# State-space inputs shifted by one step: from matrix products in the token loop to transfers ahead of it

## The reference, cut to what matters

```python
gamma = lam * dt
beta = (1.0 - lam) * dt * jnp.exp(A_disc)
X = x_heads * gamma[..., None] + jnp.pad(x_heads[:, :-1] * beta[:, 1:, :, None], ((0, 0), (1, 0), (0, 0), (0, 0)))
Y, _ = ssd_chunk(X, A_disc, Bm, Cm)
```

## Time and profile before

| | |
|---|---|
| median of 3 runs | 3973.22 us (3966.16 to 3978.81) |
| the profiled execution | 3973.28 us, its span 3971.5 us |
| PE busy | 3450.7 us, 87% |
| DVE busy | 2610.3 us, 66% |
| ACT busy | 1180.8 us, 30% |
| POOL busy | 503.4 us, 13% |
| mean granted TensorE clock | 0.914 |

### The profile page before, as it was taken

One profiled execution on the slowest core, in us unless ns is written; L12 is line 12 of the kernel. 1 busy time (PEld: TensorE's weight loads), 2 busy tenths in 40 slices (PEclk: granted clock), 3 DMA queues, 4 the chain that ended last, 5 costly groups with the idle time before them and its releaser, 6 DMA issues.

```text
span 3971.5 us, 37643 instructions
## 1 busy us (share of the span) xinstructions
PE 3450.7 (87%) x12941; PEld 2128.7 (54%) x12941; DVE 2610.3 (66%) x3732; ACT 1180.8 (30%) x1948; POOL 503.4 (13%) x404
## 2 busy tenths in 40 slices
PE   1877878878879999999999589998989898989998
PEld 0553553553555776777777346543554356434643
DVE  5877877877875777888888244664466435644563
ACT  1332332332331544333433132212222223123210
POOL 1002003003003111111111201110212011201100
PEclk9979989989989999999999797899789978998799
DMA  3202201201203878788787500231013201220011
GB/s 137 80 28 46 80 30 46 81 29 34 73 29 123 274 239 262 228 272 264 254 277 242 219 37 1 85 120 65 32 75 111 85 32 75 100 97 32 2 63 42
DMA packets 276638, 436.71 MB, mean 110 GB/s; under 512 B 52320, under 2 KB 189536, under 8 KB 263904
## 3 DMA queue, kind: packets, MB, share of 16 engines
q1 hardware_dynamic: 256768, 379.84, 28.9%
q0 software_dynamic: 19680, 54.46, 4.2%
HBM read 364.59 MB, written 93.77 MB: 115 GB/s over the span
## 4 chain that ended last, share of the span: by engine, by line
PE 61%; DVE 23%; DVEq 6%; ACT 4%; issue 2%; DMA 2%; POOL 1%; SPq 0%; ACTq 0%; POOLq 0%
PE bank L1012 11%; PE bank L1041 6%; PE bank L1283 6%; PE bank L1296 4%; PE bank L1304 4%; PE bank L1212 4%; PE bank L828 3%; PE bank L1149 3%; DVE sb_gla L1884 3%; PE bank L1190 2%; DVE sb_ratio L1859 2%; DVEq L1865 2%; PE bank L1018 2%; PE bank L1248 1%; PE bank L808 1%
## 5 line engine op out<-in xcount | busy, mean ns | idle before, releaser
L1012 PE MATMUL bank<-sb_xT,sb_work 128*128 128x256 f32 x2304 | 513.0, 382 | 1.6 <-issue 0.8
L1012 PEld LDWEIGHTS bank<-sb_xT,sb_work 128*128 128x128 f32 x2304 | 439.3, 192 | 75.2 <-issue 17.5
L828 PE MATMUL bank<-sb_gla,sb_work 128*128 128x256 f32 x896 | 260.3, 443 | 112.6 <-DVE sb_work L1886 100.0
L1041 PE MATMUL bank<-sb_work,sb_hT 128*128 128x512 f32 (+1 forms) x666 | 296.1, 592 | 0.0
L828 PEld LDWEIGHTS bank<-sb_gla,sb_work 128*128 128x128 f32 x896 | 188.9, 218 | 175.6 <-DVE sb_work L1886 121.1
L808 PE MATMUL bank<-sb_hT,sb_work 128*128 128x512 f32 x384 | 181.1, 620 | 99.6 <-DVE sb_hT L1833 99.6
L1296 PE MATMUL bank<-sb_parts,sb_gla 128*128 128x512 f32 x512 | 240.3, 613 | 4.5 <-ACT sb_gla L1628 4.5
L1304 PE MATMUL bank<-sb_parts,sb_gla 128*128 128x512 f32 x512 | 230.8, 593 | 5.9 <-DVE sb_work L2450 5.9
L1283 PE MATMUL bank<-sb_work,sb_parts 128*128 128x512 f32 x512 | 230.8, 610 | 2.8 <-ACT sb_work L1641 2.8
L1884 DVE TENSOR_TENSOR sb_gla<-sb_gla,sb_work 128x1024 f32<-128x1024 f32 x112 | 146.0, 1303 | 128.9 <-PE bank L828 122.9
L1149 PE MATMUL bank<-sb_parts,sb_hT 128*128 128x512 f32 x512 | 228.7, 605 | 0.0
(11 more groups left out here) (396 smaller groups left out, 6103.3 us busy)
## 6 DMA issues: line engine op xcount, KB each, us to landing
sb_work<-scratch_gu SPq DMA_DIRECT2D x63, 1408.0 KB, 7.5
sb_parts<-scratch_mx SPq DMA_DIRECT2D x16, 3072.0 KB, 12.1
sb_work<-moe_w SPq DMA_DIRECT2D x63, 512.0 KB, 6.7
scratch_y<-sb_work SPq DMA_DIRECT2D x48, 512.0 KB, 7.8
sb_parts<-scratch_fq SPq DMA_DIRECT2D x24, 1024.0 KB, 8.0
sb_work<-w_qkvg SPq DMA_DIRECT2D x64, 256.0 KB, 2.5
scratch_gu<-moe_w SPq DMA_DIRECT2D x32, 512.0 KB, 5.8
sb_parts<-fT SPq DMA_DIRECT2D x48, 256.0 KB, 3.4
```

Source lines behind the costliest of these rows:

```text
L828: mm = pe.matmul(dst.rearrange("p (h n l) -> p h n l", h=HPC, l=size), kS[u % 2][:, k * P:(k + 1) * P], late[:, :, k, :, 1, :], start=True ...
L1012: mm = pe.matmul(dst, egu[j % 3][:, which * NC + k, m * P:(m + 1) * P], xt[j % 2][:, k, :], start=(k == 0), stop=(k == NC - 1))
L1041: mm = pe.matmul(bank(YB[s]), einter[j % 2][0:n, a:a + P], edn[j % 3][0:n, m * D:(m + 1) * D], start=(m == 0), stop=(m == EC - 1))
```

## The change

The matrices `shift` and `edge` go, and with them the products on PE. For each batch SP issues seven transfers from buffer to buffer: for each tile k, rows 0 to 126 of `xh[k]` go to rows 1 to 127 of a new tile `late[k]`, and the last row of `xh[k]` to row 0 of `late[k + 1]`. `late[0]` and `late[1]` lie in `R[2]`, `late[2]` and `late[3]` in `R[1]`. Each pair of transfers waits for the two SiLU steps that make `xh[k]`. DVE sets row 0 of `late[0]` to zero, and ahead of the token loop waits for all seven transfers at once (`s_late`), multiplies the four tiles with beta in place, and in the loop adds `late[k]` where it added `Xd`.

```diff
@@ constant_table
-    parts["shift"] = np.eye(P, k=1)
-    edge = np.zeros((P, P))
-    edge[P - 1, 0] = 1.0
-    parts["edge"] = edge
@@ build, events and buffers
-        s_shift = ev("s_shift", NT)
+        s_late = ev("s_late", 2 * NT - 1, 16)
+        late = [R[2 - k // 2][:, (k % 2) * 1024:(k % 2 + 1) * 1024] for k in range(NT)]
@@ SP, after the store of the batch before
+                sp.wait_ge(h2_ready.sem, h2_ready.at(b, NT))
+                for k in range(NT):
+                    sp.wait_ge(s_silu.sem, s_silu.at(b, 4 * k + 2))
+                    sp.dma_start(late[k][1:P, :], xh[k][0:P - 1, :]).then_inc(s_late.sem, 16)
+                    if k + 1 < NT:
+                        sp.dma_start(late[k + 1][0:1, :], xh[k][P - 1:P, :]).then_inc(s_late.sem, 16)
@@ PE, start of tile k
-                    if k:
-                        pe.wait_ge(s_y.sem, s_y.at(b, k))
-                    for h in range(2):
-                        col = slice(h * 512, (h + 1) * 512)
-                        mm = pe.matmul(bank(h), cst("shift"), xh[k][:, col], start=True, stop=(k == 0))
-                        if k:
-                            mm = pe.matmul(bank(h), cst("edge"), xh[k - 1][:, col], start=False, stop=True)
-                    mm.then_inc(s_shift.sem, 1)
@@ DVE, set-up
                 dve.memset(state[:, :], 0.0)
+                dve.memset(late[0][0:1, :], 0.0)
@@ DVE, ahead of the token loop
+                dve.wait_ge(s_late.sem, s_late.at(b + 1, 0))
+                for k in range(NT):
+                    tt(r3(late[k], SP_), r3(late[k], SP_), bcast(tm[:, k, 1, :], SP_), ALU.mult)
+                dve.drain()
@@ DVE, tile k, after differences(0)
-                    dve.wait_ge(s_shift.sem, s_shift.at(b, k + 1))
-                    for h in range(2):
-                        tt(r3(Xd[:, h * 512:(h + 1) * 512], SP_), r3(bank(h), SP_),
-                           bcast(tm[:, k, 1, h * 8:(h + 1) * 8], SP_), ALU.mult)
-                    dve.drain()
                     dve.wait_ge(s_gx.sem, s_gx.at(b, k + 1))
-                    tt(x, x, Xd, ALU.add).then_inc(s_xg.sem, 1)
+                    tt(x, x, late[k], ALU.add).then_inc(s_xg.sem, 1)
```

## The result

The changed kernel took 4108.59 us (median of 4 runs, 4104.55 to 4110.66) against 3975.55 us for the kernel before: a ratio of 1.0339 (95% interval 1.0325 to 1.0353), 133 us slower. The forecast was 4064 us, with 4010 to 4150 as its range. The profiled execution spans 4106.6 us against 3971.5, 135.1 us more.

A forecast was written before the change was run, and what follows sets the result against it. The token loop was taken as a relay between TensorE and VectorE, neither full. A late loop start of 106.5 us less 16 us gained gives 90.5 us on 3973.28: 4064 us, range 4010 to 4150.

The forecast's parts named there:

- One engine for 127 rows: Large buffer-to-buffer transfers in set-up: 127 rows can be dealt equally over one engine only, 20.5 us each; chance 0.82.
- The price of the wait: Token loop's start: first `diagonal` late by 27.9 us in batch 0, 26.2 in the three others, 106.5 us together.
- No cover: Between set-up and token loop: nothing covers the delay, as set-up is over and the loop has no other work.
- The gain in tiles 1 to 3: Token loop: projection starts earlier without the shift and edge products; 4 us per batch taken, 16 us in all.
- The lower bound: Tiles 1 to 3: nothing gained; at the lower clock three short groups give back some 2.9 us per tile.
- The sign named for it: New profile's token loop: tiles 1 to 3 must be shorter by 1 to 3 us each.
- The upper bound: Tiles 1 to 3: projection could start 1.0, 2.7 and 2.4 us earlier, 6.1 us per batch.
- one engine at its slowest with nothing gained: Whole kernel: 22.0 us a transfer and no gain in the later tiles, 4104 us.
- the widening for the duration of a transfer: Large transfers: duration widened to 17.5 to 25.5 us, each us worth 16 us in total; range 4010 to 4150.
- The first, 16 engines: Large transfers: rows dealt unevenly over 16 engines, landing ahead of the loop; 20 us gained, 3953 us; chance 0.09.
- The second rival: Transfers and token loop: 16 engines, but the lower clock takes back the later tiles' gain; 3973 us; chance 0.03.
- The third, 40 us a transfer: Large transfers: one engine at half rate, as it reads and writes the buffer; 4376 us; chance 0.06.

## Why the prediction was right, and where not

**One engine for 127 rows.** Right. It was argued from 8 of 16 engines in line 582's transfers; 127 rows moved at a share of 0.06, one transfer behind the other, and four more row counts moved at the share of their largest divisor. The Trainium skill ("DMA: Bandwidth & Descriptors", section "Why a DMA increments its semaphore by 16 and not by 1") states that rule, and these five shares agree with it.

**The price of the wait.** 106.5 us forecast, 117.7 measured. A transfer that has its engine to itself takes 20.2 us where I took 20.5, inside the bounds of 19.9 and 22.0. The last one takes 23.3 to 23.7: the weights' first load (issued at 2376.10) shares the engine with it. That sharing was dismissed in the prediction as harmless for the weights; what it does to the last transfer was not asked. The 3.1 to 3.5 us more cover the 2.8 us per batch that are missing. The packets show the two at the same time; no run has the weights out of the way.

**No cover.** Right: the wait for the tile alone takes all of it away, with the same slow transfers.

**The gain in tiles 1 to 3.** This is the step that failed. I took 4 us per batch out of bounds of 0 and 6.1, and the loops became 1.8 us longer on average. The lower bound was argued with the clock but set too high: I bounded the clock's harm by the short groups ahead of the projection, while it also slows the projection behind them. The sign named for it, tiles 1 to 3 each 1 to 3 us shorter, did not come. The upper bound is not contradicted: with idle products in both, the loops differ by 6.2 us. A timeline of the changed kernel, batch 1, tiles 1 and 2, shows it (it answers to the earlier trace rows):

```profile
2891.37 1.97 PE L1202 MATMUL bank<-sb_const,sb_work 128*128 128x128 f32 x8 [1.86 <-ACT sb_work L1590]
2893.27 3.78 PE L1185 MATMUL bank<-sb_small,sb_const 16*128 16x128 f32 x16
2896.97 5.33 PE L1216 MATMUL bank<-sb_work,sb_parts 128*128 128x128 f32 x32
...
2923.63 1.64 PE L1202 MATMUL bank<-sb_const,sb_work 128*128 128x128 f32 x8 [0.95 <-ACT sb_work L1590]
2925.20 3.78 PE L1185 MATMUL bank<-sb_small,sb_const 16*128 16x128 f32 x16
2928.91 6.37 PE L1216 MATMUL bank<-sb_work,sb_parts 128*128 128x128 f32 x32
```

The same tiles in the kernel before.

```profile
2827.58 1.09 PE L1198 MATMUL bank<-sb_const,sb_work 128*128 128x128 f32 x8
2828.60 2.37 PE L1181 MATMUL bank<-sb_small,sb_const 16*128 16x128 f32 x16
2830.90 6.73 PE L1212 MATMUL bank<-sb_work,sb_parts 128*128 128x128 f32 x32
...
2862.32 1.09 PE L1198 MATMUL bank<-sb_const,sb_work 128*128 128x128 f32 x8
2863.34 2.05 PE L1181 MATMUL bank<-sb_small,sb_const 16*128 16x128 f32 x16
2865.32 3.84 PE L1212 MATMUL bank<-sb_work,sb_parts 128*128 128x128 f32 x32
```

In tile 2 (the lower three rows of each) transposes, broadcasts and projection took 1.09, 2.05 and 3.84 us and now take 1.64, 3.78 and 6.37: 4.8 us more for the same instructions, 2.5 of them in the projection, which the bound left out. The granted clock of that stretch was 1.00 before and is 0.56 now, near the lower of its two levels (0.50, 1.2 of 2.4 GHz); before, TensorE came to it without a wait from the products with `shift` and `edge`, and now it waits 0.95 us ahead of the transposes. As windows, before and now:

```profile
2862.30:2869.20 6.90, 6.90 (x60) 6.59 (x59) 5.64 (x6) 2.23 (x4) 3.51 (x2) 1.00 0.01 2
2923.60:2935.30 11.70, 11.67 (x59) 11.12 (x59) 2.56 (x3) 3.51 (x5) 3.76 (x2) 0.56 0.00 0
```

**The sum.** The result is 44.6 us above the forecast: 11.2 from the wait, 23.3 from the loops (16 us of gain forecast, 7.3 of loss measured), 8.0 ahead of layer 1 and 2.1 elsewhere. It is also above the 4104 worked out for one engine at its slowest with nothing gained. It lies inside the range to 4150 through the widening for the duration of a transfer, which was only a quarter of what was off (11.2 of 44.6 us): that much is luck.

**The rivals.** The first, 16 engines, could be built, and took 3992 us, not the 3953 worked out for it. Its first error is the same 4 us per batch. The second is at the loop's start, where the products with two buffer inputs took 6.33 us beside GpSimd's, for 4.63 without. The Trainium skill ("SBUF — State Buffer", section "Who interferes with whom") says that such products and GpSimd's get in each other's way, and this trace agrees. A third part, the 9.5 us ahead of layer 1, is not explained. The second rival, 16 engines with the lower clock taking the gain back (3973 us), comes nearest in the loops: no gain. The third, 40 us a transfer, is out: 20.2 were measured.

## What to carry to other kernels

Count the rows of a transfer and its largest divisor up to 16 before pricing it: 127 rows moved on one engine, 112 on all sixteen. The count of engines is not yet their rate: on four engines here each moved at half of it. A wait for all of several queued transfers costs the last of them; a wait for each costs what its own use can't hide. Where TensorE runs between the two levels of its clock, price removed work by the clock of what stays, in the whole relay behind it, and try whether a useless product in a wait pays.

## What the runs showed that was not expected

Behind a transfer on one engine, SyncE's issue of a 4 KB transfer took 8.50, 13.88 and 16.50 us, where it took 0.71, 0.89 and 0.94 us behind transfers of 112 and 15 rows. So here a transfer that itself ran on one engine held the queue that issues it. Nothing urgent stood behind it in this kernel.

Idle products on TensorE, nothing else, made the kernel before 1.0% faster (0.99), with a loop of 106.1 us at a clock of 0.86 for 114.1 at 0.72. Together with the transfers on many engines and the earlier beta it is 1.8%, with 97.1 us at 0.93.
